# Eight partial softmax sums added in pairs of heads 3 to 23, four of them by an accumulating DMA, with output and weight remainders moved up in VectorE's order

## The reference

```python
x = x + xattn(layernorm(x), ctx)            # x (4, 512, 256), ctx (4, 1024, 256)
x = x + ffn(layernorm(x))

# xattn: 16 heads of 64
q = (layer_norm(latents) @ Wq);  k, v = split(layer_norm(context) @ Wkv)
k = apply_rope(k, cos, sin)
attn = softmax(clip(einsum('bhnd,bhsd->bhns', q, k) * 64 ** -0.5, -11.0, 11.0))
out  = einsum('bhns,bhsd->bhnd', attn, v) @ Wo + bo

# ffn: 16 experts of 128
sel = sigmoid(einsum('bsd,ed->bse', x, expert_sel))
out = einsum('bseh,ehv,bse->bsv', relu(einsum('bsd,edh->bseh', x, keys)), values, sel)
```

## Time and profile before

| | |
|---|---|
| median of 3 runs | 1003.43 us |
| profiled execution | 1003.22 us |
| span of its trace | 1001.4 us |
| TensorE busy | 970.6 us (97%), granted clock 0.9 or more in every slice |
| VectorE busy | 822.3 us (82%) |
| ScalarE busy | 527.7 us (53%) |
| GpSimd busy | 145.4 us (15%) |
| DMA engines, mean share over the span | 32.5% |

### The profile page before, as it was taken

The page is one execution under the profiler, slowest core; times in us unless marked ns, Lnnn a source line. Parts: engine busy times, 40 slices in busy tenths (PEclk is TensorE's granted clock), DMA queues, the critical chain, the costliest instruction groups (busy, mean ns, idle before and its releaser), DMA issues. The chain is left out here.

```text
span 1001.4 us, 16033 instructions
## 1 busy us (share of the span) xinstructions
PE 970.6 (97%) x5712; PEld 620.4 (62%) x5712; DVE 822.3 (82%) x1275; ACT 527.7 (53%) x765; POOL 145.4 (15%) x130
## 2 busy tenths in 40 slices
PE   4999999999999999999999999999999989999998
PEld 3655555555555555555555555555555368898898
DVE  8888899998999999999999988999888876545422
ACT  4666556565665656665666655555555542222221
POOL 3200000000000000000000000321000054445443
PEclk9999999999999999999999999999999999999999
DMA  7343323332323323233333223322222472242331
GB/s 220 111 134 96 111 85 111 101 96 74 102 68 97 90 75 90 75 99 96 92 85 100 66 85 85 85 85 85 86 64 66 137 273 76 95 128 92 117 108 42
DMA packets 66553, 99.77 MB, mean 100 GB/s; under 512 B 19824, under 2 KB 42608, under 8 KB 64432
## 3 DMA queue, kind: packets, MB, share of 16 engines
q1 hardware_dynamic: 66480, 98.82, 32.5%
HBM read 70.01 MB, written 10.75 MB: 81 GB/s over the span
## 5 line engine op out<-in xcount | busy, mean ns | idle before, releaser
L1144 ACT ACTIVATE wide_a<-score_ps 128x1024 f32<-128x1024 f32 x256 | 248.6, 1024 | 116.0 <-PE score_ps L894 115.9
L1448 DVE TENSOR_SCALAR wide_a<-wide_a 128x1024 f32<-128x1024 f32 x256 | 171.1, 698 | 37.4 <-ACT wide_a L1144 37.2
L1457 DVE TENSOR_TENSOR p_sum<-wide_a 128x1024 f32<-128x1024 f32 x128 | 158.3, 1237 | 2.3
L907 PE MATMUL o_ps<-wide_a,v_sb 128*64 128x512 f32 x512 | 124.0, 605 | 1.8 <-issue 1.8
L907 PE MATMUL o_ps<-wide_a,values_a 128*64 128x512 f32 x512 | 124.0, 605 | 1.0 <-issue 1.0
L894 PE MATMUL score_ps<-q_hi,k_hi 64*128 64x512 f32 x512 | 114.6, 444 | 1.8 <-DVE k_lo L1441 1.0
L1994 DVE SCALAR_TENSOR_TENSOR act<-h_ps,wide_a 128x512 f32<-128x512 f32 x62 | 42.7, 689 | 87.0 <-PE h_ps L153 81.6
L894 PEld LDWEIGHTS score_ps<-q_hi,k_hi 64*128 64x128 f32 x512 | 47.8, 183 | 104.8 <-issue 70.6
L1916 ACT CAST act_hi<-act 128x512 fp32r<-128x512 f32 x64 | 39.7, 621 | 137.9 <-DVE act L1994 135.4
L894 PE MATMUL score_ps<-q_hi,k_lo 64*128 64x512 f32 x512 | 101.1, 391 | 0.0
L894 PE MATMUL score_ps<-q_lo,k_hi 64*128 64x512 f32 x512 | 100.3, 388 | 0.0
(11 more groups left out here) (230 smaller groups left out, 1965.1 us busy)
## 6 DMA issues: line engine op xcount, KB each, us to landing
wide_a<-sel_dram SPq DMA_DIRECT2D x16, 1024.0 KB, 4.8
k_swap<-k SPq DMA_DIRECT2D x124, 128.0 KB, 2.4
w_hi<-packs_hi SPq DMA_DIRECT2D x26, 384.0 KB, 3.0
w_lo<-packs_lo SPq DMA_DIRECT2D x26, 384.0 KB, 3.6
den<-inv_dram SPq DMA_DIRECT2D x64, 128.0 KB, 2.8
ctx_raw<-ctx SPq DMA_DIRECT2D x24, 128.0 KB, 2.3
packs_hi<-w_hi SPq DMA_DIRECT2D x8, 384.0 KB, 3.0
packs_lo<-w_lo SPq DMA_DIRECT2D x8, 384.0 KB, 3.7
```

The lines of the kernel that those rows point to most:

```text
L907: mm = pe.matmul(o_ps[DH * h:DH * h + DH, :], v_sb[n // 2 % 2][:, at:at + DH], probs[s % RING][:, h, :], start=(s == 0), stop=(s == STEPS ...
L1144: act.activation(probs[s % RING][:], score_ps[s % 2][:], ACT.Exp, scale=DH ** -0.5).then_inc(exp_done, 1)
L1448: dve.tensor_scalar(probs[s % RING][:], probs[s % RING][:], CLIP_HI, CLIP_LO, ALU.min, ALU.max).then_inc(clipped, 1)
L1457: dve.tensor_tensor(p_sum[m][:], first, second, ALU.add).then_inc(summed_up, 1)
```

## The change

1. `EIGHTS` is now pairs 3 to 23, so pairs 3 to 7 add all eight steps too.
2. In all pairs of `EIGHTS` the first of the three further additions (p_sum 0 into p_sum 1) is no longer VectorE's. GpSimd issues a DMA that reads both and adds (`add_four`), as soon as `sum_up(n, 1)` is done. `sum_six` waits for its landing on a new semaphore, `four_added`.
3. `split_o` stands, in every pair from 2 on, ahead of `add_y` and `sum_up` in `m == 0`; before, in pairs 2 to 8 and 25 to 28 it stood behind the statistics of the next context tile, or behind `sum_up` where there is none.
4. `split_weights(n + 2)` stands right behind `split_k` in `m == 2`; before, it stood behind `scale_o` and `sum_quad`.

```diff
-EIGHTS = range(PAIRS, 24)
+EIGHTS = range(3,24)
...
-            return sum(1 if i in THREE_PARTS else 3 if i in EIGHTS else 2 for i in range(min(n, NPAIR - 2) + 1))
+            return sum(1 if i in THREE_PARTS else 2 for i in range(min(n, NPAIR - 2) + 1))
...
+            def add_four(n):
+
+                pool.wait_ge(summed_up, MACROS * n + 2)
+                pool.dma_start(p_sum[1][:], p_sum[0][:], accum_op=ALU.add).then_inc(four_added, DMA)
...
+                if n in EIGHTS:
+                    add_four(n)
...
             def sum_six(n):
 
-                dve.wait_ge(quads_up, quads(n) - 2)
+                dve.wait_ge(four_added, DMA * (EIGHTS.index(n) + 1))
                 dve.wait_ge(summed_up, MACROS * n + 4)
...
-                    if m == 0 and (n >= NPAIR - 3 or n - 1 in EIGHTS):
+                    if m == 0 and n >= 2:
                         split_o(dve, sh, n - 2, n % 2)
...
-                        if 2 <= n < NPAIR - 3 and n - 1 not in EIGHTS:
-                            split_o(dve, sh, n - 2, n % 2)
...
                         if p < NPAIR:
                             split_k(p)
+                        if n + 2 < PAIRS:
+                            split_weights(n + 2)
...
-                        if not last:
+                        if not last and n not in EIGHTS:
                             sum_quad(n, 0)
-                        if n + 2 < PAIRS:
-                            split_weights(n + 2)
```

More of the change, by code:

```diff
@@ L430, in attention_phase @@
         quads_up = sem("quads_up")
+        four_added = sem("four_added")
         pv_done = sem("pv_done")
```

## The result

| | before | after |
|---|---|---|
| median of 6 runs each, same chip | 1004.44 us (1002.45 to 1006.26) | 999.60 us (997.68 to 1000.32) |
| profiled execution, span | 1003.22, 1001.4 us | 999.90, 998.1 us |
| TensorE, VectorE, GpSimd busy | 970.6, 822.3, 145.4 us | 968.8, 806.7, 162.6 us |

The ratio is 0.9941, with a 95% interval of 0.9914 to 0.9967: 4.8 us less. A second measurement of the changed kernel, on another chip, gave 999.69 us against 1005.28, ratio 0.9943 (0.9923 to 0.9963), with a span of 995.5 us in its profiled execution. The forecast was 997.4, its own range 994.5 to 1000.5, the wider range stated with it 994.0 to 1006.0. The span of a trace and the median of several runs are two measures: from trace to trace the gain is 3.3 us (1001.4 to 998.1), or 5.9 with the second trace (995.5, from the other chip).

What follows compares the result with a forecast made beforehand. TensorE, busy 970.6 of 1001.4 us, was taken as the bound, with VectorE close behind. Gains 1.41 + 2.7 + 0.26 + 2.15 + 0.2 less 0.8 gave 5.9 us, so 997.4 us; own range 994.5 to 1000.5, wider 994.0 to 1006.0.

Steps and rivals of the forecast that it cites:

- Weight remainders: Pair 2: the remainder moved up ends TensorE's idle time before a k projection; gain 1.41 us.
- Output remainders: Pairs 3 to 6: the earlier remainder removes four waits with no named releaser before the products with v; gain 2.7 us.
- The 0.26 us for the wait of the denominators in pair 3: Pair 3: the denominators' wait of 1.09 us for a sum shrinks by 0.26 us through both moves.
- The loss in pairs 25 to 27: The early output remainder delays the sums before the denominators there; loss 0.8 us, bounds 0 and 1.7.
- Narrower denominators: Pairs 3 to 7 go to the 256-column form, 0.43 us less each; gain 2.15 us.
- The addition by DMA: Pairs 8 to 23: off TensorE's path, lands in 6.5 to 7.5 us, no wait of `sum_six`; gain 0.2 us.
- X: Delay of the denominators' spread beside the DMA addition; taken as 0.9 us, bounds about -1 and 3.
- The stall of 1.5 us: In pair 10 the spread was 1.93 us late and the next denominators waited 1.5 us; to shrink by 0.2.
- The spread behind the addition: Slower rival, pairs 3 to 23: spread queues behind the addition, X = 2.5 costs about 17 us, 1014.5; chance 0.17.
- Nearly nothing: Rival, pairs 2 to 8: VectorE becomes the bound and gains turn into other waits, 1001.3 us; chance 0.18.
- The late addition: Rival: the DMA addition lands too late, 12 us to landing costs TensorE 27 us, so 1024; chance 0.03.

Runs made afterwards that it cites:

- e3: The kernel before with only the addition by DMA, in its own pairs 8 to 23, old order elsewhere: 1006.64 us, ratio 0.9992.
- e2: The kernel before with only the two moves in VectorE's order (output remainder and weight remainder earlier): 999.98 us, ratio 0.9922.
- e4: The changed kernel with the output remainder of pairs 25 to 28 back behind the sum, as before: 1000.16 us, ratio 0.9934.
- e1: The changed kernel with the first addition of pairs 3 to 23 back on VectorE, no DMA addition: 999.03 us, ratio 0.9918.
- f1: The changed kernel with scale_o behind the fourth pair sum and the addition back on VectorE: 996.17 us, ratio 0.9913.
- e7: The changed kernel with a second DMA behind each addition, writing the first partial sum (512 KB) to DRAM: 1014.91 us, ratio 1.0084.
- e6: The changed kernel with the addition by DMA issued only after the spread has landed, its result wanted last: 995.67 us, ratio 0.9895.
- f2: The changed kernel with both scale_o behind the fourth pair sum and the DMA addition behind the spread: 997.18 us, ratio 0.9915.
- f3: f2 with the second lot of keys split by VectorE and not by GpSimd: 995.51 us, ratio 0.9908.
- f4: f2 with the sums of eight by DMA in pairs 3 to 28, no longer 3 to 23: 994.29 us, ratio 0.9894.
- e5: The changed kernel with VectorE's scale_o moved behind the fourth pair sum: 995.31 us, ratio 0.9892.

## Why the prediction was right, step by step

*Weight remainders.* Right: pair 2 is 1.44 us shorter (1.41 forecast), and the row before the k projection is gone.

*Output remainders.* The list of the change puts `split_o` ahead of `add_y` in every pair; in pairs 4 to 24 it stands behind `sum_all` and `add_y` and ahead of `sum_up` only. The gain doesn't hang on it: the remainder ends 6.5 us earlier in pair 3 (counted from the pair's start; I had said 3) and 1.5 to 2.7 us earlier in pairs 4 to 8. The 2.7 us were right, and with them the reading that the unnamed releaser was the remainder: the four waits stay in e3, without the moves, and are gone in e2, with them alone. The 0.26 us for the wait of the denominators in pair 3 was mis-sized: all 1.09 us went. The sum started 1.5 us earlier in its pair (109.01 - 103.48 = 5.53 us after its start, 7.03 before), and I had counted only the order of that pair, not that VectorE had entered it late: its first clip began 2.09 us after the pair's start, and now at it. Against that stands a wait of 0.36 us in pair 4 that no step had, behind the late store of pair 2.

*The loss in pairs 25 to 27.* Forecast 0.8; e4 shows 0.6, all of it in pair 27. The stretch lost 1.0 us in the second trace. The 0.35 us in pair 25 doesn't come from the remainder, since it stays in e4 (and in e3, with the old order, it is larger). The 4.55 us of the first trace are a late store and the collision with GpSimd in one pair, and the half clock behind them (1.45 us), which no term had. A late store and the collision were in the kernel before too, apart (the collision at 685.90, 3.31 us long).

*Narrower denominators.* Right by the traces: pairs 7 and 8 are 0.50 and 0.44 us shorter, and TensorE has 1.8 us less to do. No timed run shows the 2.15 us by themselves; e1, which has them, and e2, which has not, are 0.95 us apart, inside their spread.

*The addition by DMA.* Right that it is off TensorE's path, brings next to nothing by itself (0.3 us less in pairs 9 to 24 in one trace, 0.3 more in the other; e3, and e1 and f1 without it), and never makes `sum_six` wait. Its duration was mis-sized: 4.9 us to landing and not 6.5 to 7.5, under my lower bound of 5.4 from the plain copy. The estimates from the Trainium skill (DMA: Bandwidth & Descriptors, Anatomy of one DMA — SWDGE (gpsimd) path), 3.2 us for the bytes once and 4.4 for twice, would have been nearer: the second is 0.5 us short of the median measured. X was 0.7 us, forecast 0.9.

*The stall of 1.5 us.* I took the earlier trace rows for a spread beside other transfers. It was a late store, which the prediction didn't know of.

*The sum.* 5.9 us forecast, 4.8 and 5.6 measured; the second trace's span is 995.5 us, as forecast. That it came out so near is in part luck. Pairs 2 to 8 gave 7.4 us where their terms add up to 6.5, and what was lost behind them was more than forecast: waits behind late stores in five pairs and not one, and in the first trace the half clock. That the moves alone measured 6.3 us (e2), as much as the whole, shows how little a sum that is right to 1 us says about its single terms.

*The rivals.* The spread behind the addition: priced rightly (e7), but X stayed under its threshold. Its way in, GpSimd held up by clips (the rule of the Trainium skill, SBUF — State Buffer, Who interferes with whom), was not put to the test by the changed kernel: the clips of the row that the prediction cites run 7.8 us after the issue (398.56 against 390.77), and in all 21 pairs of the first trace the issue, 0.86 to 1.10 us long, falls beside no clip. Where it does, in e6, f2, f3 and f4, GpSimd is held up as the rule has it, by up to 1 us. Nearly nothing: refuted, pairs 2 to 8 give 7.4 us. The late addition: refuted by 4.9 us (5.6 at most in the first trace) against a window of 9.3.

## What to carry to other kernels

When a row of waits has no releaser, look for the instruction that ends within a tenth of a us before it and for the engine that idles behind that one; moving it was worth at least the wait here (2.7 us of 2.7, and 1.44 of 1.41). Where an in-order engine has one instruction that waits for a chain of DMAs, put it as late as its result allows: this one line (e5) was worth nearly as much again as the whole change (4.4 us), and its runs agreed within 1.3 us. An operation moved from a busy engine to a DMA costs the transfers beside it something; ask how much slack they had, since the price is small up to that and then comes in every iteration (e7). And take a change apart before crediting its most striking part: here two moved lines measured as much as the whole (e2), and the DMA by itself nothing (e3).

## What the runs showed of the hardware

- An accumulating DMA of 512 KB within SBUF, issued by GpSimd, takes 0.9 us of GpSimd and lands in 4.6 to 5.6 us (both traces of the changed kernel; 4.4 to 6.8 over all runs). Beside VectorE's clips the issue takes up to 1.9 us (f2). It makes a 128 KB broadcast from DRAM beside it 0.6 to 0.7 us later; with a second 512 KB transfer to DRAM behind it, 2.4 us.
- An addition of VectorE with two operands in SBUF (1.22 us) takes 3.3 to 3.4 us beside a 128x1024 subtraction of GpSimd, which itself takes 2.4 us alone and up to 3.2 so, and a clip of 0.69 us takes 1.7 to 2.9. VectorE's operation ends 1.1 or 0.55 us after GpSimd's, by how long it takes alone. The Trainium skill (SBUF — State Buffer, Who interferes with whom) says that a VectorE instruction with two inputs in SBUF contends with a GpSimd instruction that reads SBUF; the trace agrees, and in f3, where VectorE does both, neither is held up.
- A 4 KB store to DRAM took 3.0 to 3.9 us in all 20 cases in which a 16 KB instruction packet started 0.6 to 1.2 us behind its issue, and 1.39 or 1.40 in all 21 with one at 1.25 to 1.45 us. A packet was not moved on purpose, so that it is the cause is not shown.
- TensorE's granted clock fell to half for 3.41 us behind waits of 3.27, 1.78 and 1.84 us (first trace, e1, e2) and cost 1.45 to 1.8 us each time; behind waits of 2.60, 2.08 and 1.92 us it did not fall.
